# Layer 1 of a four-layer kernel: four-lane products without queries, a mask compared by words, earlier weight loads and moved clears

## The chip, the cores and the metric

One Trainium2 chip, one core. The metric is the device time of one execution in microseconds (us), taken as the median of repeated runs. Everything is float32 except the mask (one byte per entry) and a few integers.

## The reference, cut to what matters

The program updates x (2 batches of 1024 tokens with 256 features) four times, each time by x = x + ffn(cond(x)). Layers 0, 2 and 3 are mixtures of experts. Only layer 1 and some clears of memory are touched. Layer 1 is attention with 16 heads of 16 features, in which one query per head serves every token:

```
q, k, v = x @ Wq.T, x @ Wk.T, x @ Wv.T        (heads h of 16)
tp   = t @ Wt.T                               (t: 256 per batch)
a    = sum_e tp[b,h,e] * q[b,h,s,e]
qmod = sum_s a[b,h,s] * q[b,h,s,:]            (one vector per b, h)
scores[b,h,t,s] = where(mask[t,s], qmod.k[s] / 4, float_min)
c = (softmax(scores) @ v) @ Wo.T
```

After it comes a block with 16 experts: a gate (normalised c times a normalised 256x16 matrix, minus a sigmoid, rectified, softmax), per-expert q, k and v, causal attention, and an output product weighted by the gate. In the inputs all 1024 rows of the mask are equal. Then every token of a batch has the same c, attention over equal rows gives that row back, and layer 1 adds one row of 256 numbers per batch to x.

## The kernel before, in words

Tokens are held twice in SBUF: `xtok` (128 tokens by 16 tiles by 256) and `fx` (the 256 features as 2 halves `k` of 128 partitions, by 2048 tokens). Both are views into one tensor, `big`, of six regions (`ACC`, `EXTRA` and so on). PSUM is `ps`, 8 banks of 128x512. A stage is a Block: a list of instructions for each engine, ordered among each other by semaphores. `with_own_semaphores` (L2561) puts a barrier, a clearing of semaphores and a second barrier behind a part.

Start: `stage_load` (L103). SyncE (SP) loads x and small tables and waits for nine of the loads. ScalarE (ACT) waits for the same nine, then issues three DMAs (L127) that write zeros to all 4992 rows (5.1 MB) of the DRAM scratch `sorted_in`, and one (L129) for one row of `by_token`. `sorted_in` is first used when layer 2 scatters tokens into it (`scatter`, L1421).

Layer 0 ends in `half_l0` (L1429). Its SP list ends with four loads of results, and one load of layer 2's first weights once the old ones are used (L1465).

Layer 1 (`layer1`, L2569) has these stages:

- `stage_l1_project` (L1822). SP loads the mask (8 tiles of 128x1024 bytes), its first row spread to all partitions, and five weight matrices (1.3 MB). PE makes tp (L1863), then q for all tokens (L1871, 16 calls of 512 columns), then a, spread over each head's features by a block-diagonal weight (L1880, 8 calls). ACT copies q out of PSUM (L1898). VectorE (DVE) compares the mask byte by byte with its first row and counts (L1907, L1909, 8 times each), then multiplies and sums q and a (L1923). With the weights of k, qmod becomes U (L1890), a 256-vector per batch and head, so that scores are U.x. The count of differing bytes goes to `differ` (L1940).
- A branch on `differ`. If it is 0, `stage_l1_same_rows` (L2381) runs; the general path (`any_mask`) isn't executed.
- `stage_l1_same_rows` is three Blocks. The first: scores for one batch at a time on 16 partitions (L2428), maximum, exp, transposes (L2435), probabilities times x (L2442), then the products with Wv (L2458) and Wo (L2464). The second is `stage_l1_gating` (L2090): it loads two small tables (L2114, L2115), takes four products and runs some thirty short DVE operations. The third: 32 calls with the experts' value weights as stationary operand and two columns moving (L2523), 32 more with the output weights (L2529), then the row is spread (L2550, L2535) and added to `fx` (L2553) and `xtok` (L2558) by DVE.

The expert weights (4 MB) are issued by SP in the first of these Blocks (L2413, L2414). PE's list is in order, as is each engine's; `link` (L335) makes DVE wait for its own last instruction.

## Time and profile before

| what | value |
|---|---|
| time, median of 3 runs | 1822.16 us (1815.49 to 1824.17) |
| time of the profiled execution | 1827.07 us |
| its span, first to last instruction | 1825.3 us |
| PE, DVE, ACT, POOL busy | 84%, 56%, 36%, 23% of the span |
| mean granted clock of TensorE | 0.905 of full |
| mean DMA rate | 116 GB/s |

The profile is of one execution. PE is TensorE, PEld its weight loads, POOL is GpSimd; L1871 is line 1871 of the kernel. "SPq" and "ACTq" mark the time in which a queue's engine issues a DMA, not the transfer. A float32 matmul call stands as two records, so "x64" in the row of a product means 32 calls; a transpose is one record. The end of a matmul is modelled, so ends of one product and starts of the next overlap.

### The profile page before, as it was taken

How to read it: one execution, taken by the hardware profiler on the slowest of the kernel's cores; microseconds unless marked ns; L12 is line 12 of the kernel's file. 1: busy time of each engine (PE TensorE's matmuls, PEld its weight loads, DVE VectorE, ACT ScalarE, POOL GpSimd, SP SyncE). 2: the span in 40 equal slices, each digit the busy share in tenths (PEclk: the TensorE clock that was granted, in tenths of full speed). 3: DMA queues.
4: the chain of work that ended last, by engine and by line, in shares of the span. 5: the costliest groups of instructions: out<-in, count | busy, mean ns of one | idle time of the engine just before them, and what ended most of it. 6: DMA issues, size and time to landing. Idle time of an engine off the chain costs nothing. (4 is left out here: it accounts for less than half of the span.)

```text
span 1825.3 us, 26214 instructions
## 1 busy us (share of the span) xinstructions
PE 1533.0 (84%) x8442; PEld 1164.3 (64%) x8442; DVE 1013.2 (56%) x1801; ACT 661.3 (36%) x981; POOL 428.0 (23%) x364
## 2 busy tenths in 40 slices
PE   3788878866689999879799999999988699848993
PEld 2553323733668778768688888888776577725662
DVE  2737767452263435473577777776546133536675
ACT  1337767211032333242455555554323133211110
POOL 0412222000034241001033334342003334023321
PEclk9989989886579999989899999999997699959996
DMA  6328981213031334024022221300303232245733
GB/s 200 137 93 331 364 310 58 84 55 93 23 137 62 103 101 150 1 81 162 3 90 99 94 97 57 134 28 14 133 1 130 101 99 79 95 142 203 265 109 107
DMA packets 82585, 211.11 MB, mean 116 GB/s; under 512 B 10561, under 2 KB 57426, under 8 KB 74258
## 3 DMA queue, kind: packets, MB, share of 16 engines
q1 hardware_dynamic: 61568, 160.98, 24.8%
q0 software_dynamic: 15840, 43.27, 7.0%
q10 hardware_dynamic: 5042, 5.11, 0.8%
q8 instruction: 78, 1.28, 0.3%
q14 instruction: 57, 0.47, 0.1%
HBM read 164.90 MB, written 44.43 MB: 115 GB/s over the span
## 5 line engine op out<-in xcount | busy, mean ns | idle before, releaser
L593 POOL DMA_INDIRECT results<-sb_big,sb_s_out_row x63 | 132.8, 2108 | 465.1 <-ACT sb_big L824 303.1
L898 DVE TENSOR_TENSOR sb_h_split<-sb_big,sb_h_split 128x2048 fp32r<-128x2048 f32 x78 | 178.5, 2290 | 87.9 <-ACT sb_h_split L893 87.9
L893 ACT CAST sb_h_split<-sb_big 128x2048 fp32r x78 | 146.6, 1903 | 41.9 <-issue 40.6
L789 PE MATMUL ps<-sb_big,sb_e_hT 128*128 x624 | 141.0, 379 | 1.1 <-DVE sb_e_hT L942 1.1
L282 PE MATMUL ps<-sb_h_split 128*128 128x512 f32 x312 | 133.6, 428 | 9.6 <-DVE sb_h_split L917 6.8
L1031 DVE COPY sb_g_space<-sb_big 128x1024 f32 x168 | 108.4, 699 | 47.0 <-DMA sb_big<-in_l_routed 24.9
L1031 ACT COPY sb_g_space<-sb_big 128x1024 f32 x120 | 118.7, 1050 | 41.7 <-DMA sb_big<-in_l_routed 32.4
L1421 POOL DMA_INDIRECT sorted_in<-sb_big,sb_p_slots x64 | 70.6, 1104 | 260.6 <-DVE sb_p_slots L1247 216.8
L789 PEld LDWEIGHTS ps<-sb_big,sb_e_hT 128*128 128x128 f32 x624 | 118.2, 190 | 18.5 <-issue 1.3
L282 PE MATMUL ps<-sb_g_split,sb_g_ws 128*128 128x512 f32 x256 | 109.6, 428 | 23.3 <-DVE sb_g_product L461 15.7
L284 PE MATMUL ps<-sb_h_split 128*128 128x512 f32 x312 | 124.1, 398 | 0.0
L283 PE MATMUL ps<-sb_h_split 128*128 128x512 f32 x312 | 123.9, 397 | 0.0
L1069 PE MATMUL ps<-sb_g_space,sb_e_rT 128*32 128x512 f32 x768 | 99.9, 640 | 18.3 <-ACT sb_g_space L1031 8.5
L555 POOL DMA_INDIRECT results<-sb_big,sb_p_out_row x78 | 77.6, 995 | 145.3 <-DVE sb_big L704 144.6
L283 PE MATMUL ps<-sb_g_split,sb_g_ws 128*128 128x512 f32 x256 | 107.3, 419 | 0.0
L284 PE MATMUL ps<-sb_g_split,sb_g_ws 128*128 128x512 f32 x256 | 106.5, 416 | 0.0
L282 PE MATMUL ps<-sb_g_ws,sb_g_split 128*128 128x256 f32 x256 | 79.6, 311 | 26.1 <-DVE sb_g_split L467 18.5
L582 POOL DMA_INDIRECT sb_big<-by_token,sb_s_in_row x63 | 64.5, 1025 | 153.0 <-DVE sb_s_out_row L1294 134.4
L436 ACT ACTIVATE sb_g_sg<-ps 128x512 f32<-128x512 f32 x64 | 38.2, 598 | 157.0 <-PE ps L284 108.8
L636 PE MATMUL ps<-sb_big,sb_x_rT 128*128 x312 | 87.5, 403 | 4.1 <-ACT sb_x_rT L681 4.0
L461 DVE TENSOR_TENSOR sb_g_product<-sb_g_sg,ps 128x512 f32<-128x512 f32 x64 | 43.8, 685 | 70.8 <-ACT sb_g_sg L436 54.2
L656 PE MATMUL ps<-sb_big,sb_x_hT 128*128 x312 | 82.1, 386 | 0.0
(416 smaller groups left out, 3318.6 us busy)
## 6 DMA issues: line engine op xcount, KB each, us to landing
sb_big<-in_l_routed SPq DMA_DIRECT2D x32, 1024.0 KB
sb_big<-in_l2f_routed SPq DMA_DIRECT2D x8, 3072.0 KB, 11.1
sb_e_wring<-in_l_experts SPq DMA_DIRECT2D x16, 1408.0 KB
sb_big<-in_l_routed SPq DMA_DIRECT2D x32, 512.0 KB
sb_big<-results SPq DMA_DIRECT2D x32, 512.0 KB, 7.4
sb_big<-sorted_in SPq DMA_DIRECT2D x18, 512.0 KB
by_token<-sb_big SPq DMA_DIRECT2D x12, 512.0 KB, 3.6
sorted_in<-sb_big ACTq DMA_DIRECT2D x2, 2048.0 KB
```

What stands on the lines that cost most here:

```text
L282: pe.matmul(to, w[0], x[0], start=start, stop=False)
L283: pe.matmul(to, w[0], x[1], start=False, stop=False)
L284: return pe.matmul(to, w[1], x[0], start=False, stop=stop)
L555: pool.indirect_dma_start(out=results, out_offset=bass.IndirectOffsetOnAxis(ap=places.out_row[:, j:j + 1], axis=0), in_=self.tile(j), in_o ...
L593: pool.indirect_dma_start(out=results, out_offset=bass.IndirectOffsetOnAxis(ap=places.out_row[:, j:j + 1], axis=0), in_=self.tile(j), in_o ...
L636: last = pe.matmul(psum[:, j % 2, 0:self.NF * P], self.rT[:, j % 2, k * P:(k + 1) * P], self.w[:, e, k * self.NF * P:(k + 1) * self.NF * P ...
L656: last = pe.matmul(psum[:, 2 + j % 2, 0:D], self.hT[:, j % 2, f * P:(f + 1) * P], self.w[:, e, lo:lo + D].rearrange("p s n -> p (s n)"), s ...
L789: last = pe.matmul(psum[:, 7, 0:D], self.hT[:, f // TPC, f % TPC * P:(f % TPC + 1) * P], self.weight(place, 2 * KD * self.F + f * D, D), s ...
L893: act.copy(self.own[part][:, 0, :], self.raw(e, part)).then_inc(self.own_high[part], 1)
L898: dve.tensor_tensor(self.own[part][:, 1, :], self.raw(e, part), self.own[part][:, 0, :], ALU.subtract).then_inc(self.own_low[part], 1)
L1031: last = copy(self.own[part][:, g, :], here.rearrange("p s n -> p (s n)"))
L1069: last = pe.matmul(psum[g * W:(g + 1) * W, 2 * part + u % 2, :], self.rT[:, r % 2, k, g * W:(g + 1) * W], self.own[part][:, g, lo:lo + FU] ...
```

## The change

- The clears of `sorted_in` leave the start and go to SP's list in the first stage of layer 1, from a 128x256 tile of zeros that is read again for every tile of rows. Only the `by_token` row is still cleared at the start. Layer 2's POOL waits for the clears before it scatters; layer 0 waits for one clear instead of four.
- `half_l0` also loads layer 1's weights (now six matrices, Wq in both orientations, 1.5 MB) into `EXTRA`, and the mask as 32-bit words with its first row into `ACC`, behind the four loads of results.
- `stage_l1_project` forms no q. With V = Wq'tp per head, a = V.x; then r = sum of a[s] x[s], and qmod = Wq r, masked by head. Both big products use four quadrants of the array (32 weight columns each), every quadrant with its own 512 tokens. The mask is compared in two DVE instructions of 128x2048 words and summed in one.
- `stage_l1_same_rows` is one Block. Scores, probabilities times x, and both expert products use the quadrants; in the expert products the vectors (padded to 32 columns) are the weights and the expert matrices move. Each batch's softmax is now in two halves that are joined by DVE. ACT takes half of the adds to `fx`.

The core of the diff:

```diff
@@ stage_load @@
                     act.wait_ge(cleared, 1)
-                    act.wait_ge(loaded, 16 * 9)
-                    for lo in range(0, SLOT_TILES2, NT):
-                        hi = min(SLOT_TILES2, lo + NT)
-                        act.dma_start(sorted_in[lo * P:hi * P, :].rearrange("(i p) d -> p i d", p=P),
-                                      acc[:, 0:hi - lo, :]).then_inc(zeroed, 16)
                     act.dma_start(by_token[0:1, :], acc[0:1, 0, :]).then_inc(zeroed, 16)
...
-                    dve.memset(acc, 0.0).then_inc(cleared, 1)
+                    dve.memset(acc[0:1, 0, :], 0.0).then_inc(cleared, 1)
@@ half_l0, SP and POOL @@
+                        sp.dma_start(l1_weights, a["l1_w"]).then_inc(l1_in, 16)
+                        sp.dma_start(l1_words[:, 0:TPB, :], a["mask_words"].rearrange("(i p) s -> p i s", p=P)
+                                     ).then_inc(l1_mask, 16)
+                        sp.dma_start(l1_words[:, TPB, :], a["mask_words"][0, :].partition_broadcast(P)).then_inc(l1_mask, 16)
...
-                        pool.wait_ge(zeroed, 16 * (1 + -(-SLOT_TILES2 // NT)))
+                        pool.wait_ge(zeroed, 16)
@@ half_cond, POOL @@
+                        if n == 2:
+                            pool.wait_ge(swept, 16 * 3)
@@ new helpers @@
+        def in_lanes(pe, to, w, bank):
+
+            for k in range(KD):
+                for g in range(NCH):
+                    last = pe.matmul(psum[g * EQ:(g + 1) * EQ, bank, :], w[:, k, :], fx[:, k, g * CH:(g + 1) * CH],
+                                     start=(k == 0), stop=(k == KD - 1))
+            last.then_inc(to, 1)
+
+        def lanes_times_rows(pe, to, turned, bank):
+
+            for q in range(TPC):
+                for g in range(NCH):
+                    last = pe.matmul(psum[g * EQ:(g + 1) * EQ, bank, 0:D], turned[:, q, g * EQ:(g + 1) * EQ],
+                                     xtok[:, g * TPC + q, :], start=(q == 0), stop=(q == TPC - 1))
+            last.then_inc(to, 1)
+
+        def turn_lanes(pe, to, lanes, n, bank):
+
+            for q in range(n):
+                last = pe.transpose(psum[:, bank, q * P:(q + 1) * P], lanes[:, q * P:(q + 1) * P], ident[:])
+            last.then_inc(to, 1)
@@ stage_l1_project @@
+                        sp.wait_ge(blank, 1)
+                        for lo in range(0, SLOT_TILES2, NT):
+                            n = min(SLOT_TILES2 - lo, NT)
+                            sp.dma_start(sorted_in[lo * P:(lo + n) * P, :].rearrange("(i p) d -> p i d", p=P),
+                                         zero[:].unsqueeze(1).to_broadcast([P, n, D])).then_inc(swept, 16)
...
+                        pe.wait_ge(tpmd, 2)
+                        for d in range(KD):
+                            for o in range(KD):
+                                last = pe.matmul(psum[:, 6, d * BH:(d + 1) * BH], w6[:, WQT, o, d * P:(d + 1) * P],
+                                                 tpm[:, o, :, :].rearrange("p b h -> p (b h)"),
+                                                 start=(o == 0), stop=(o == KD - 1))
+                        last.then_inc(vd, 1)
+                        pe.wait_ge(vc, 1)
+                        in_lanes(pe, ad, V, 0)
+                        pe.wait_ge(ac, 1)
+                        turn_lanes(pe, atd, lanes, TPC, 1)
+                        pe.wait_ge(atc, 1)
+                        lanes_times_rows(pe, rd, aT, 2)
+                        pe.wait_ge(rc, 1)
+                        turn_lanes(pe, rtd, r, KD, 3)
+                        pe.wait_ge(rbd, 1)
+                        for o in range(KD):
                             for k in range(KD):
+                                last = pe.matmul(psum[:, 4, o * BH:(o + 1) * BH], w6[:, WQ, k, o * P:(o + 1) * P],
+                                                 rb[:, k, :, :].rearrange("p b h -> p (b h)"),
+                                                 start=(k == 0), stop=(k == KD - 1))
+                        last.then_inc(qd, 1)
+                        pe.wait_ge(qmd, 2)
                         for d in range(KD):
+                            for o in range(KD):
+                                last = pe.matmul(psum[:, 5, d * BH:(d + 1) * BH], w6[:, WK, o, d * P:(d + 1) * P],
+                                                 qm[:, o, :, :].rearrange("p b h -> p (b h)"),
+                                                 start=(o == 0), stop=(o == KD - 1))
                         last.then_inc(ud, 1)
+                        pe.wait_ge(counted, 1)
+                        pe.matmul(psum[0:1, 7, 64:65], ones[:, 0:1], cnt[:], start=True, stop=True).then_inc(flagd, 1)
...
+                        dve.wait_ge(l1_mask, 32)
+                        link(dve.tensor_tensor(ne[:], words[:, 0:TPB, :], words[:, TPB:TPB + 1, :].to_broadcast(
+                            [P, TPB, S // 4]), ALU.bitwise_xor))
+                        dve.wait_ge(atd, 1)
+                        dve.tensor_copy(aT[:].rearrange("p q g -> p (q g)"), psum[:, 1, :]).then_inc(atc, 1)
+                        link(dve.tensor_scalar(apart[:], ne[:].rearrange("p i s -> p (i s)"), 0, None, ALU.not_equal))
+                        dve.wait_ge(rtd, 1)
+                        link(dve.tensor_copy(rT[:].rearrange("p k g -> p (k g)"), psum[:, 3, 0:KD * P]))
+                        for b in range(B):
+                            two = of_batch(rT[:], b)
+                            last = dve.tensor_tensor(rb[:, :, b, :], two[:, :, 0, :], two[:, :, 1, :], ALU.add)
+                        last.then_inc(rbd, 1)
...
+                        dve.tensor_reduce(cnt[:], apart[:], AX_X, ALU.add).then_inc(counted, 1)
@@ stage_l1_same_rows @@
+                    for g in range(NCH):
+                        sp.dma_start(m1[g * EQ:(g + 1) * EQ, :],
+                                     a["mask"][0, g % 2 * CH:(g % 2 + 1) * CH].partition_broadcast(EQ)).then_inc(masked, 16)
+                    sp.dma_start(simc[:, :, 0:E], a["l1_sim"]).then_inc(simmed, 16)
+                    sp.dma_start(gb[:], a["l1_gates"].partition_broadcast(P)).then_inc(simmed, 16)
+                    for k in range(KD):
+                        sp.dma_start(wv[:, :, k, :], a["l1_qkv"][:, :, k, 2 * H1:3 * H1]).then_inc(wloaded, 16)
+                    sp.dma_start(wo[:], a["l1_o"]).then_inc(wloaded, 16)
...
+                    pe.wait_ge(expd, 1)
+                    turn_lanes(pe, ptd, pr, TPC, 1)
+                    pe.wait_ge(sread, 2)
+                    pe.matmul(psum[:, 4, 0:2 * P], ones[:], spread[:].rearrange("p n q -> p (n q)"), start=True, stop=True
+                              ).then_inc(spreadd, 1)
+                    pe.wait_ge(ptc, 1)
+                    lanes_times_rows(pe, zd, pT, 2)
+                    pe.wait_ge(zc, 1)
+                    turn_lanes(pe, ztd, z, KD, 3)
...
+                    pe.wait_ge(wloaded, 48)
+                    for k in range(KD):
+                        for g in range(4):
+                            last = pe.matmul(psum[g * EQ:(g + 1) * EQ, 6, :], c32[:, k, :], wv[:, 4 * g:4 * g + 4, k, :],
+                                             start=(k == 0), stop=(k == KD - 1))
+                    last.then_inc(vd, 1)
+                    pe.wait_ge(vsd, 1)
+                    pe.matmul(psum[:, 5, 256:256 + B], vs[:], sel[:], start=True, stop=True).then_inc(vtd, 1)
+                    pe.wait_ge(avd, 2)
+                    for n in range(4):
+                        for g in range(4):
+                            last = pe.matmul(psum[g * EQ:(g + 1) * EQ, 7, 0:D], av[:, 4 * g + n, :], wo[:, 4 * g + n, :],
+                                             start=(n == 0), stop=(n == 3))
+                    last.then_inc(outd, 1)
...
+                    act.wait_ge(simmed, 32)
+                    act.activation(gb[:], gb[:], ACT.Sigmoid).then_inc(rooted, 1)
+                    act.wait_ge(maxd, 1)
+                    act.activation(pr[:], pr[:], ACT.Exp, bias=mx[:, 0:1], accum_out=sums[:, 0:1]).then_inc(expd, 1)
+                    act.wait_ge(shared, 1)
+                    act.activation(share[:], share[:], ACT.Exp).then_inc(weighed, 1)
```

## Rows read from the trace of the kernel before

**Rows 1.** Busy by stretch: length, PE, PEld, DVE, ACT, POOL, PEclk, DMA share, GB/s.
```profile
371.80:412.00 40.20, 27.38 (x74) 13.55 (x74) 27.41 (x46) 4.69 (x8) 0.69 (x2) 0.79 0.18 63
...
413.40:444.20 30.80, 25.81 (x92) 11.45 (x92) 6.16 (x18) 3.76 (x5) 0.09 (x1) 0.72 0.44 137
444.20:459.90 15.70, 4.45 (x20) 4.34 (x20) 6.02 (x32) 4.60 (x7) 0.00 (x0) 0.50 0.02 3
459.90:496.20 36.30, 28.72 (x132) 28.17 (x132) 8.38 (x12) 0.00 (x0) 0.00 (x0) 0.50 0.00 0
...
497.50:1825.30 1327.80, 1165.65 (x5864) 950.28 (x5864) 755.78 (x1351) 465.50 (x704) 353.77 (x282) 0.92 0.29 100
```

**Rows 2.** Timeline of the start: start us, duration us, engine, line, what, idle before.
```profile
11.11 11.33 ACTq L127 DMA_DIRECT2D sorted_in<-sb_big  x3
22.47 2.09 ACTq L129 DMA_DIRECT2D by_token<-sb_big  x1
25.75 1.28 ACT L187 ACT_TABLE_LOAD   x1 [25.75 <-PEq L2567]
```

**Rows 3.** Timeline of the first stage of layer 1.
```profile
381.83 1.87 PE L1863 MATMUL ps<-sb_condT,sb_l_w 128*128 128x2 f32 x8 [12.23 <-DMA sb_l_w<-in_l_w]
...
411.86 0.14 DVE L1940 CAST sb_l_differ<-sb_l1p_cnt 1x1 int32<-1x1 f32 x1
```

**Rows 4.** Groups of layer 1: count, busy us, mean ns, idle before.
```profile
L2523 PE MATMUL ps<-sb_f_c,sb_f_wbuf 128*128 128x2 f32 x64 | 13.8, 352 | 7.8 <-PEq L2111 7.8
...
L1907 DVE TENSOR_TENSOR sb_l1p_ne<-sb_l1p_m 128x1024 f32<-128x1024 uint8 x8 | 9.8, 1224 | 7.0 <-DMA sb_l1p_m<-in_mask 6.7
L1909 DVE TENSOR_REDUCE sb_l1p_cnt<-sb_l1p_ne 128x1 f32<-128x1024 f32 x8 | 9.8, 1220 | 0.3
...
L1880 PE MATMUL ps<-sb_big,sb_l_bd 128*128 128x512 f32 x16 | 7.1, 597 | 0.8 <-ACT sb_big L1898 0.8
...
L1923 DVE CUSTOM_DVE_ANT_0 sb_l_junk<-sb_big,ps 128x512 f32<-128x512 f32 x8 | 5.5, 689 | 3.2 <-PE ps L1880 3.2
L1898 ACT COPY sb_big<-ps 128x512 f32<-128x512 f32 x8 | 4.7, 586 | 25.7 <-PE ps L1871 25.7
L2558 DVE TENSOR_TENSOR sb_big<-sb_big,ps 128x2048 f32<-128x2048 f32 x2 | 4.5, 2280 | 0.0
...
L2553 DVE TENSOR_SCALAR sb_big<-sb_big,sb_f_row 128x1024 f32<-128x1024 f32 x4 | 2.7, 747 | 0.0
...
L2535 PE MATMUL ps<-sb_ident,sb_f_rowb 128*128 128x128 f32 x4 | 1.1, 435 | 0.7 <-DVE sb_f_rowb L2550 0.7
```

**Rows 5.** Timeline, products in four quadrants in layers 0 and 2.
```profile
60.35 1.92 PE L298 MATMUL ps<-sb_big,sb_wr 128*32 128x512 f32 x16 [0.92 <-PEq L191]
...
142.39 1.93 PE L1093 MATMUL ps<-sb_g_space,sb_r_quads 128*32 128x256 f32 x32 [0.19 <-issue]
...
501.56 3.41 PE L298 MATMUL ps<-sb_big,sb_wr2c 128*32 128x512 f32 x16
```

**Rows 6.** Timeline of the second stage of layer 1.
```profile
444.61 0.43 SPq L2115 DMA_DIRECT2D sb_g1s_gb<-in_l_gates  x1
447.71 0.22 ACT L2139 ACTIVATE sb_g1s_gb<-sb_g1s_gb 128x16 f32<-128x16 f32 x1 [1.90 <-DMA sb_g1s_gb<-in_l_gates]
...
452.96 0.25 DVE L2161 RECIPROCAL sb_g1s_ns<-sb_g1s_ns 128x16 f32<-128x16 f32 x1 [0.38 <-ACT sb_g1s_ss L2142]
...
459.48 0.19 DVE L2185 TENSOR_TENSOR sb_f_rw<-sb_g1s_tmp,sb_g1s_small 128x32 f32<-128x32 f32 x1
```

**Rows 7.** Busy by stretch, during the clears.
```profile
12.40:24.40 12.00, 0.00 (x0) 0.00 (x0) 0.00 (x0) 0.00 (x0) 0.00 (x0) 1.00 1.05 365
```

**Rows 8.** Timeline of SyncE's queue at the end of layer 0.
```profile
325.03 0.60 SPq L1465 DMA_DIRECT2D sb_wbuf<-in_l2c_shared  x1
```

**Rows 9.** Timeline of ScalarE in layer 0: a table load and its user.
```profile
70.88 1.28 ACT L436 ACT_TABLE_LOAD   x1
72.17 1.09 ACT L436 ACTIVATE sb_g_sg<-ps 128x512 f32<-128x512 f32 x2
```

More of the change, by code:

```diff
@@ L1841, in stage_l1_project @@
+                cnt = sb("l1p_cnt", [P, 1], on=own)
+                zero = sb("l1p_zero", [P, D], on=own)
+                blank, masks, order, tpd, tpmd, vd, vc, ad, ac, atd, atc, rd, rc, rtd, rbd, qd, qmd, ud, counted, flagd = (
+                    sem("l1p_" + n) for n in ("blank", "masks", "order", "tpd", "tpmd", "vd", "vc", "ad", "ac", "atd", "atc", "rd",
+                                              "rc", "rtd", "rbd", "qd", "qmd", "ud", "counted", "flagd"))
                 with nc.Block() as block:
@@ L1900, in _ @@
+                        act.wait_ge(rd, 1)
+                        act.copy(r[:], psum[:, 2, 0:D]).then_inc(rc, 1)
                     @block.vector
                     def _(dve):
-                        dve.memset(qm[:], 0.0)
-                        dve.wait_ge(mloaded, 32)
-                        for i in range(TPB):
-                            if i:
-                                dve.wait_ge(counted, 2 * i)
-                            dve.tensor_tensor(ne[:], m8[:, i, :], m1[:], ALU.not_equal).then_inc(counted, 1)
-                            dve.wait_ge(counted, 2 * i + 1)
-                            dve.tensor_reduce(cnt[:, i:i + 1], ne[:], AX_X, ALU.add).then_inc(counted, 1)
+                        link = chain(dve, order)
@@ L1926, in _ @@
-                        dve.wait_ge(asum, 8)
-                        dve.tensor_tensor(qmod[:], part[:, :, :, 0], part[:, :, :, 1], ALU.add).then_inc(order, 1)
-                        dve.wait_ge(order, 2)
-                        for o in range(KD):
-                            for b in range(B):
-                                last = dve.tensor_scalar(qm[:, o, b, o * 8:(o + 1) * 8], hm[:, :, 0],
-                                                         qmod[:, o, b:b + 1], float(HW) ** -0.5, ALU.mult, ALU.mult)
@@ new lines, in stage_l1_same_rows @@
+            E, BH = E1, B * HEADS
+            wv = sb("f1_wv", [P, E, KD, H1], on=own)
+            wo = sb("f1_wo", [P, E, D], on=own)
+            m1 = sb("f1_m1", [P, CH], U8, on=own)
+            lim = sb("f1_lim", [P, CH], on=own)
+            pr = sb("f1_pr", [P, CH], on=own)
+            pT = sb("f1_pT", [P, TPC, P], on=own)
+            mx, sums = (sb("f1_" + n, [P, 1], on=own) for n in ("mx", "sums"))
+            spread = sb("f1_spread", [P, 2, P], on=own)
+            peak, total, share, tmp2 = (sb("f1_" + n, [P, B, 2, HEADS], on=own) for n in ("peak", "total", "share", "tmp2"))
@@ new lines, in stage_l1_same_rows @@
+            cb = sb("f1_cb", [P, KD, B, P], on=own)
+            c32 = sb("f1_c32", [P, KD, EQ], on=own)
+            ss, top, small = (sb("f1_" + n, [P, B], on=own) for n in ("ss", "top", "small"))
+            L, tmp, oh1, oh2, gated, rw, rwm = (
+                sb("f1_" + n, [P, B, E], on=own) for n in ("L", "tmp", "oh1", "oh2", "gated", "rw", "rwm"))
+            rwl = sb("f1_rwl", [P, 4], on=own)
+            sel = sb("f1_sel", [P, B], on=own)
+            selb = sb("f1_selb", [P, B, P], on=own)
```

489 lines of the change are left out of this document (234 added, 255 removed).

## The prediction

> **What bounds the kernel now.** I first read the busy time by stretch, which cuts the span where one stage gives way to the next. Layer 1 is the piece from 371.8 to 497.5 us, 125.7 us in all, and the 1327.8 us behind it begin only when its last add is done [rows 1]. So layer 1 is serial: whatever it loses comes off the end. PE looks busy in it, but with little: from 444 to 496 us the granted clock is 0.50, the lower of its two levels (1.2 GHz). Then the timeline of the start: ACT issues the three clears from 11.11 to 22.44 us and the `by_token` row until 24.56, and layer 0 starts at 25.75, 1.2 us behind that [rows 2]. Nothing computes between. Then the timeline of the first stage: the first product, at 381.83, waits 12.2 us for its weights, and the last cast ends at 412.0 [rows 3]. Last the groups of layer 1: q and the expert products, plus the byte compares and counts (8 + 8 of 1.22 us, 19.6 us of DVE) that hold up tp and with it a [rows 4].
>
> **The change, part by part.**
>
> *Start.* The nine loads had landed at 11.11, when ACT went on [rows 2]. SP still waits for them; ACT's one small clear takes 2.09 us beside it and its memset is shorter. With the same 1.2 us of barrier layer 0 starts at 12.3: **-13.4 us**.
>
> *First stage, now 40.2 us* [rows 1]. Weights and mask have landed (below). Prices: a product of 4 calls (8 records) with full weights and few columns is 1.87 us [rows 3], as are 64 records in 13.8 us [rows 4]. A four-quadrant product, 16 records of 512 columns, has two prices: 1.92 us at the upper clock, 3.41 at the lower; 32 records of 256 columns are 1.93 at the upper, so about 3.5 at the lower [rows 5]. I take the lower clock throughout: the products here are short with waits between, as in the second half of the layer before, where it read 0.50 [rows 1]. A pass over 512 columns of PSUM is 0.59 us on ACT and 0.69 on DVE; four transposes with their tail are 1.1 at that clock [rows 4]. A short DVE step is 0.2 [rows 6].
> The chain: four small products 7.6; the two big ones 3.4 + 3.5; copies 0.6 + 0.7; four transposes 1.1 and two 0.6; two 256-column copies 0.8; eight short DVE steps 1.6; behind U the count, U's copy and the flag 1.0. Sum 20.9, so **-19.3 us**.
> The mask is three DVE instructions of 2048 columns. The nearest rows are the add of 2048 columns, 2.28, and the reduction of 1024, 1.22 [rows 4]. The xor (2.3) has 5 us of cover (in_lanes, ACT's copy, the transposes). The compare (1.3 to 2.3) stands between aT's copy and rT's, with 4.5 us of cover; the count (2.3) has U's product (1.9) beside it. Uncovered they would cost up to 6 us; nothing speaks for a gain.
> The clears are on SP's queue here. Their issue took ACTq 11.33 us [rows 2]; the stage's barrier comes at 20.9, so it is hidden. The data, 5.1 MB, moved at 365 GB/s before [rows 7], 14 us; the next user of SP's queue is the mask row of the second stage, at 22. Nothing then waits. POOL's new wait in layer 2 stands before all its scatters, but comes over 60 us after the issue of the clears; it costs nothing unless they take that long.
>
> *Prefetch.* SP's last issue of layer 0 is at 325.03 [rows 8], 47 us before layer 1. Three more DMAs with 2.7 MB in front of it take 7.4 us at 365 GB/s [rows 7]. They stand behind the results, so these aren't late. Cost nothing; without that cover they would give back the wait for the weights.
>
> *Second stage, now 82.8 us in three Blocks* [rows 1]. (a) SP issues four mask rows and sim, 0.4 each, then gates, whose data is used 3.1 us after the issue [rows 6]: 5.4. ACT's list has the Sigmoid first, so Exp waits for gates: Sigmoid 0.2, table load 1.3, exp 0.6 + 0.2: 7.7, where scores alone would have let it start at 5.6. This is the new wait; the softmax, all of PE and the rest are behind it. (b) Transposes 1.1, copy 0.7, spread operand and its product 1.2, product with x 3.5, z's copy 0.4, two transposes 0.6: 7.5. The joining of the halves (DVE, about nine short steps) lies beside the product with x. (c) z joined 0.7, Wv 1.9, masking 0.4, Wo 1.9, three copies 0.8, logits 1.9, two steps and the square roots 0.75: 8.35. (d) The gating chain, 452.96 to 459.67, is 6.7 [rows 6], plus two steps: 7.15. The value product (3.4) runs beside it, its weights long there. (e) Weighting and sum 1.4, the turn 0.3, two steps 0.5, output product 3.5, copy 0.4, rows turned 0.95, copy 0.2: 7.25. (f) Two adds to fx of 0.68 (4 in 2.7 us) and two to xtok of 2.28 [rows 4]: 5.9; ACT's two lie beside. With 0.4 for the branch's tail: 44.2, so **-38.6 us**. The barriers between stages stay.
>
> By the Trainium skill (ScalarE: Activation LUTs, What ACT_TABLE_LOAD costs) a switch costs about 2.66 us with a drain, of which the load is 1.28. In layer 0 a load at 70.88 has its user at 72.17, 1.29 later [rows 9], so the row speaks for 1.3; by the page (a) would be 1.4 us longer. The same skill (TensorE: Matmul & The Clock Gate, Measured speedup vs the span model) gives 3.07x for four row tiles and 2.38x for three column tiles. Here sixteen 512-column records in a line took 7.1 us [rows 4] and in quadrants 1.92 [rows 5], 3.7x; by 3.07x each of the four big products on the path would be some 0.8 us longer, 3 us in all.
>
> **Sum.** 13.4 + 19.3 + 38.6 = 71.3 us. Against the profiled execution's own 1827.07 that is 1755.8; that execution is 4.9 us above the median of the runs, and against 1822.16 it is 1750.9. I take **1751**. Layers 2 and 3 are unchanged; their 1327.8 us only start earlier.
>
> **Rivals.**
> 1. *The upper clock.* If PE kept its upper clock (2.4 GHz) through layer 1, each of the four big products on the path would save 1.5, and each of the seven small ones at most half of its 1.9: up to 12.6, so 1738 to 1743. For: the first stage now reads 0.79 on average [rows 1]. Against: the 0.50 from 444 on, and PE has more gaps after the change. Chance 0.10.
> 2. *The covers are short.* The mask work stays on DVE's path (6), Exp's wait and the many hand-overs cost more than the short steps show (some 45 links at 0.1 to 0.2, 4 to 9), or a big product is slower than in layer 2. That gives 1761 to 1766. For: word-wise xor and compare have no row. Against: the hand-overs in [rows 6] are priced in. Chance 0.20.
> 3. *Slower: the clears block SP's queue.* They read one zero tile again and again, which no row shows, and the second stage's loads stand behind them on the same queue. In the free case gates land 27.7 us after the first stage's start. If the 5.1 MB need longer, all of the second stage waits. At 100 GB/s (the mean behind layer 1 [rows 1]) they take 51 us: Exp starts 24 us late, 1775. The gain is used up at 98 us, 52 GB/s; at 40 GB/s they take 128 us, 1851. Against: the same row size ran at 365. Chance 0.07 for a delay that shows, 0.03 for slower than before.
> 4. *It doesn't do what it says.* If the word compare counted a difference, the general path would run, slower by far than 1822. An xor of equal words is 0. Chance 0.01.
>
> **The numbers.** A measurement of this kernel tells about 0.5%, 9 us, from no change. Forecast 0.60, rivals 0.10, 0.20, 0.07 (0.03 of it slower), 0.01, and 0.02 for something that leaves no difference. Faster is 0.94, same 0.02, slower 0.04. The range runs from 1738, the whole of rival 1, to 1768, rival 2's 15 us (6 + 9) and 2 us of scatter.
>
> **What would show it.** Layer 0's first transpose at 12.3; layer 1's first product at once, with no wait for weights; the first stage 20.9 us long with PEclk 0.5; SP's three clears issued within 12 us; Exp's wait ending at 7 us with the gates as its releaser; second stage 44 us; layer 2's first scatter without a wait. It is wrong if SP's queue or the DMA rate shows the clears still moving in the second stage, if a DVE row of 2048 words stands between two PE products with PE idle, or if the part behind layer 1 isn't 1328 us.

## The result and the profile after

The changed kernel takes 1749.13 us (median of 4 runs, 1748.79 to 1754.33), the kernel before beside it 1823.16 (4 runs, 1815.49 to 1827.36). The ratio is 0.9606, with a 95% interval of 0.9576 to 0.9636: 74 us less, against 71.3 forecast. The profiled execution has a span of 1752.6 us.

The busy time by stretch of the changed kernel, cut as in [rows 1]: layer 0, the two stages of layer 1, and all behind them (length, PE, PEld, DVE, ACT, POOL, PEclk, DMA share, GB/s):

```profile
12.20:355.90 343.70, 280.67 (x2260) 156.31 (x2261) 205.17 (x335) 183.01 (x257) 72.27 (x65) 0.92 0.54 194
355.90:377.50 21.60, 16.86 (x88) 10.17 (x88) 8.31 (x17) 0.96 (x2) 0.92 (x3) 0.50 0.67 237
379.00:423.60 44.60, 25.71 (x142) 12.96 (x142) 20.63 (x72) 9.89 (x15) 0.61 (x2) 0.58 0.32 97
423.60:1752.60 1329.00, 1166.07 (x5864) 950.73 (x5864) 755.68 (x1351) 464.90 (x704) 353.50 (x282) 0.92 0.29 100
```

Measured from event to event (layer 0's first table load; the first DVE instruction of layer 1; the end of the flag's cast; the first table load behind it; the end of the last add; the first DMA issue of layer 2):

| us | before | after | difference | forecast |
|---|---|---|---|---|
| start | 25.75 | 12.19 | -13.56 | -13.4 |
| layer 0 | 346.18 | 343.76 | -2.42 | 0 |
| first stage | 40.07 | 21.55 | -18.52 | -19.3 |
| second stage | 82.73 | 44.59 | -38.14 | -38.6 |
| two gaps (barrier, branch) | 2.81 | 3.24 | +0.43 | 0 |
| behind | 1327.76 | 1327.27 | -0.49 | 0 |
| span | 1825.3 | 1752.6 | -72.7 | -71.3 |

The three stretches that the change touches account for 70.2 us of the 72.7. Layer 0's 2.4 us are within its scatter: in the runs below, where its code is the same, its length lies between 339 and 346 us, and that of the part behind layer 1 between 1315 and 1330. The two stages of layer 1 repeat to some tenths in the three traces of the changed kernel, so the experiments are read by them first and by the time second. The kernel before has one trace only.

The timeline of the changed kernel's start, ScalarE with its queue (start, duration, engine, line, what, idle before), then SyncE's queue from the end of layer 0 to layer 2:

```profile
1.80 0.48 ACTq L126 DMA_DIRECT2D by_token<-sb_big  x1
12.19 1.28 ACT L184 ACT_TABLE_LOAD   x1 [12.19 <-PEq L2659]
```

```profile
311.11 0.50 SPq L1461 DMA_DIRECT2D sb_big<-in_l_w  x1
...
356.21 7.92 SPq L1879 DMA_DIRECT2D sorted_in<-sb_l1p_zero  x3
379.29 1.75 SPq L2455 DMA_DIRECT2D sb_f_m<-in_mask  x4
...
381.70 0.59 SPq L2458 DMA_DIRECT2D sb_f_gb<-in_l_gates  x1
```

The 11 us of issue that stood before layer 0 [rows 2] are gone, and the clears' issue on SP's queue is over in 7.9 us, 15 us before the masks are asked for. Layer 2's first scatter, at 451.39, waits for its row numbers from VectorE and not for the clears. The timeline of the first stage, TensorE and the mask work of VectorE:

```profile
355.91 1.84 PE L1897 MATMUL ps<-sb_condT,sb_big 128*128 128x2 f32 x8 [2.60 <-PEq L2659]
...
360.47 2.28 DVE L1953 TENSOR_TENSOR sb_l1p_ne<-sb_big 128x2048 int32<-128x2048 int32 x1
360.61 3.64 PE L1829 MATMUL ps<-sb_big,sb_l_V 128*32 128x512 f32 x16 [0.32 <-DVE sb_l_V L1951]
...
366.79 1.22 DVE L1957 TENSOR_SCALAR sb_l1p_apart<-sb_l1p_ne 128x2048 f32<-128x2048 int32 x1
366.92 3.64 PE L1837 MATMUL ps<-sb_big,sb_l_aT 128*32 128x256 f32 x32 [0.85 <-DVE sb_l_aT L1956]
...
374.79 2.28 DVE L1972 TENSOR_REDUCE sb_l1p_cnt<-sb_l1p_apart 128x1 f32<-128x2048 f32 x1
374.93 1.91 PE L1925 MATMUL ps<-sb_l_qm,sb_big 128*128 128x32 f32 x8 [0.35 <-DVE sb_l_qm L1967]
```

The first product waits for no weights, where 12.23 us of idle time stood before it [rows 3]. Each of the three mask instructions has a product beside it; only the count (2.28 us) outlasts its product (1.91). The timeline of the second stage, where it was priced:

```profile
383.95 0.15 DVE L2554 TENSOR_SCALAR sb_f_mx<-sb_f_mx 128x1 f32<-128x1 f32 x1
384.86 0.21 ACT L2528 ACTIVATE sb_f_gb<-sb_f_gb 128x16 f32<-128x16 f32 x1 [4.57 <-DMA sb_f_gb<-in_l_gates]
385.10 1.28 ACT L2530 ACT_TABLE_LOAD   x1
386.39 0.72 ACT L2530 ACTIVATE sb_f_pr<-sb_f_pr,sb_f_mx 128x512 f32<-128x512 f32 x1
387.26 1.11 PE L1844 MATMUL ps<-sb_ident,sb_f_pr 128*128 128x128 f32 x4 [1.53 <-ACT sb_f_pr L2530]
...
395.45 1.06 PE L2488 MATMUL ps<-sb_f_zT,sb_big 128*128 128x16 f32 x8 [0.78 <-DVE sb_f_zT L2585]
...
402.33 0.25 DVE L2607 RECIPROCAL sb_f_ns<-sb_f_ns 128x16 f32<-128x16 f32 x1 [0.38 <-ACT sb_f_ss L2537]
...
409.36 0.69 DVE L2636 TENSOR_TENSOR sb_f_vw<-ps,sb_f_rwl 128x512 f32<-128x512 f32 x1
...
412.41 3.64 PE L2515 MATMUL ps<-sb_f_wo,sb_f_av 128*32 128x256 f32 x32 [0.67 <-DVE sb_f_av L2642]
...
417.79 1.42 DVE L2647 TENSOR_SCALAR sb_big<-sb_big,sb_f_row 128x1024 f32<-128x1024 f32 x2
419.12 4.48 DVE L2651 TENSOR_TENSOR sb_big<-sb_big,ps 128x2048 f32<-128x2048 f32 x2
```

The new wait of part (a) is there as named: the maxima are ready at 384.1, the Exp runs at 386.39, behind gates, Sigmoid and a table load.

### The profile page after: what moved, and what is told of

Read it like the earlier page. It is cut to its first block and busy times, and to the rows that moved or that the text cites. A ratio compares the mean times of both kernels' runs of the same rounds, so it can differ in the third digit from the quotient of the medians.

```text
span 1752.6 us, 25999 instructions
## 1 busy us (share of the span) xinstructions
PE 1489.3 (85%) x8354; PEld 1130.2 (64%) x8354; DVE 990.9 (57%) x1782; ACT 658.8 (38%) x978; POOL 429.6 (25%) x366
## 5 line engine op out<-in xcount | busy, mean ns | idle before, releaser
L1418 POOL DMA_INDIRECT sorted_in<-sb_big,sb_p_slots x64 | 70.2, 1096 | 220.7 <-DVE sb_p_slots L1244 178.4
L1066 PE MATMUL ps<-sb_g_space,sb_e_rT 128*32 128x512 f32 x768 | 97.1, 624 | 13.7 <-issue 6.4
L279 PE MATMUL ps<-sb_g_ws,sb_g_split 128*128 128x256 f32 x256 | 77.8, 304 | 21.4 <-DVE sb_g_split L464 14.5
L433 ACT ACTIVATE sb_g_sg<-ps 128x512 f32<-128x512 f32 x64 | 38.1, 597 | 148.0 <-PE ps L281 116.6
L280 PE MATMUL ps<-sb_g_ws,sb_g_split 128*128 128x256 f32 x256 | 76.8, 300 | 7.5 <-issue 7.5
```

Source lines behind the costliest of these rows:

```text
L279: pe.matmul(to, w[0], x[0], start=start, stop=False)
L280: pe.matmul(to, w[0], x[1], start=False, stop=False)
L1066: last = pe.matmul(psum[g * W:(g + 1) * W, 2 * part + u % 2, :], self.rT[:, r % 2, k, g * W:(g + 1) * W], self.own[part][:, g, lo:lo + FU] ...
L1418: pool.indirect_dma_start(out=table, out_offset=bass.IndirectOffsetOnAxis(ap=slots[:, n:n + 1], axis=0), in_=rows[:, n % NT, :], in_offset ...
```

## The experiments

Twelve kernels ran, in three groups of four; each group has its own chip and its own runs of the kernel before (1810.66, 1822.98 and 1809.31 us), so times are compared within a group and ratios across. Stage lengths come from each run's trace, by the marks of the table above.

| | us (median) | ratio, 95% | first stage | second stage |
|---|---|---|---|---|
| the change, again | 1743.38 | 0.9630 (0.9607 to 0.9652) | 21.54 | 44.29 |
| clears at the start | 1753.15 | 0.9694 (0.9675 to 0.9713) | 21.55 | 44.51 |
| late loads | 1753.75 | 0.9678 (0.9655 to 0.9701) | 32.30 | 43.93 |
| old second stage | 1777.69 | 0.9817 (0.9795 to 0.9838) | 21.55 | 76.77 |
| old expert products | 1764.69 | 0.9682 (0.9660 to 0.9704) | 21.55 | 57.19 |
| clears three times | 1767.88 | 0.9702 (0.9670 to 0.9733) | 21.55 | 45.84, and 13.7 of wait before it |
| no comparison | 1753.14 | 0.9606 (0.9584 to 0.9627) | 21.14 | 44.36 |
| filled waits | 1749.47 | 0.9601 (0.9575 to 0.9626) | 19.25 | 39.02 |
| exp first | 1741.23 | 0.9630 (0.9604 to 0.9656) | 21.55 | 41.68 |
| three moves | 1736.92 | 0.9592 (0.9567 to 0.9618) | 17.66 | 42.59 |
| filled moves | 1737.86 | 0.9612 (0.9584 to 0.9639) | 18.71 | 37.62, and 1.35 more of gap |
| the change, a third time | 1743.51 | 0.9643 (0.9619 to 0.9667) | 21.55 | 44.50 |

**The change, again.** The same file, as the measure of its group.

> The changed kernel once more, nothing edited. All of my terms are stage lengths of one trace each; this run says how far a stage length moves by itself. Serial-sum theory: start 12.2 us, first stage of layer 1 21.6, second 44.6, each within 0.3 us, median within 3 us of 1749. Layer 0 was 2.4 us shorter after the change (343.7 against 346.1), which no term explains: if that is scatter, layer 0 moves by a microsecond or more here too; if it is an effect of the change (no clears beside its start), it stays at 343.7.

It repeats, in both stages to 0.3 us. Layer 0 took 342.20 us, so it moves by itself. The median missed the 3 us expected around 1749: on this chip both kernels are faster, and the change saves 67.3 us; in the third group it saves 65.8. Both are below the 70.2 us of the three stretches. Why isn't shown, as the kernel before was not traced there; its own stages may move (see the old second stage below).

**Clears at the start.** The clears go back to ScalarE's queue ahead of layer 0, with the whole of `acc` set to zero for them, and layer 0 waits for them again.

```diff
+                    act.wait_ge(loaded, 16 * 9)
+                    for lo in range(0, SLOT_TILES2, NT):
+                        act.dma_start(sorted_in[lo * P:hi * P, :]..., acc[:, 0:hi - lo, :]).then_inc(swept, 16)
...
-                            sp.dma_start(sorted_in[lo * P:(lo + n) * P, :]..., zero[:]...).then_inc(swept, 16)
```

> The changed kernel with the three clears back on ScalarE's queue at the start, all else as changed. Serial-sum theory: layer 0 starts at 25.7 us instead of 12.2 and the time is 13.5 us above the changed kernel's, 1762.6; the first stage of layer 1 stays 21.6 us, since the clears are hidden there. Rival (the clears are not free in layer 1): the first stage and the start of the second become shorter by 1 to 5 us, and the time rises by only 8 to 12. Layer 0: 346 us if the clears slow it, 343.7 if they don't.

The timeline of ScalarE and its queue at the start of this run:

```profile
11.15 11.72 ACTq L129 DMA_DIRECT2D sorted_in<-sb_big  x3
...
25.67 1.28 ACT L189 ACT_TABLE_LOAD   x1 [25.67 <-PEq L2662]
```

Layer 0 starts 13.6 us later (25.67 against 12.08), while the first stage is 21.55 long either way. So the clears cost their whole issue ahead of layer 0 and nothing in layer 1. The time differs by 9.8, not 13.6, which lies in the range of the rival; the rival's reason, shorter stages in layer 1, is out by their lengths (21.55 and 44.51). In this profile layer 0 was 5.2 us shorter (337.05) than in the run before, the shortest of all runs. Whether that is scatter or something that the edit does isn't shown.

**Late loads.** Weights and mask words are loaded where the first stage begins, the clears behind them.

```diff
-                        sp.dma_start(l1_weights, a["l1_w"]).then_inc(l1_in, 16)
...
+                        sp.dma_start(l1_weights, a["l1_w"]).then_inc(l1_in, 16)
                         sp.wait_ge(blank, 1)
```

> The changed kernel with the mask words and the six weight matrices loaded at the start of layer 1, mask first, and the clears behind them, as the old order of loads was. Serial-sum theory: the first product waits some 10 us (the old one was issued behind 1.1 MB of mask and waited until 10.0 us into the stage; now 1.5 MB of weights), all else behind it is unchanged: plus 10 to 12 us, 1760 to 1761. The clears end later, at 28 us or so, when the stage of 32 us is still on, so they add nothing. Rival (the loads would have been hidden, or the clears share the engines with them): plus under 5, or plus 20 and more.

The timeline of SyncE's queue in its first stage, then TensorE's first product:

```profile
356.60 0.43 SPq L1875 DMA_DIRECT2D sb_big<-in_l_w  x1
357.08 14.88 SPq L1879 DMA_DIRECT2D sorted_in<-sb_l1p_zero  x3
```

```profile
366.32 1.87 PE L1897 MATMUL ps<-sb_condT,sb_big 128*128 128x2 f32 x8 [13.01 <-DMA sb_big<-in_l_w]
```

The wait for the weights is back, and the first stage is 10.8 us longer, all of it ahead of the first product; the time rises by 10.4. The clears' issue takes 14.88 us behind 2.7 MB of loads instead of 7.92.

**Old second stage.** The second stage and the gating of the kernel before, with everything else of the change kept.

```diff
-                    in_lanes(pe, sd, U[:].rearrange("p k b h -> p k (b h)"), 0)
+                                    last = pe.matmul(psum[0:HEADS, 2 * b + ch, :], U[:, k, b, :],
...
-                    lanes_times_rows(pe, zd, pT, 2)
+                                last = pe.matmul(psum[0:HEADS, 6 + b, 0:D], pT[:, b, s * HEADS:(s + 1) * HEADS],
...
+                with nc.Block() as block:
+                                last = pe.matmul(psum[:, 0, e * B:(e + 1) * B], wv[:, e, k, :], c[:, k, :],
```

> The changed kernel with the old three Blocks of the second stage (scores on 16 partitions, gating in a Block of its own, experts' weights stationary with two columns moving), all else as changed. Serial-sum theory: the second stage is 82.8 us again instead of 44.6, the time 38 us higher, 1787. Its four product groups alone (9.7, 9.8, 13.8, 13.8 us) against 3.6 each make 32 of it. Rival (the clears, which now end just before, or a lower clock on entry, slow the old form too): more than 40.

34.3 us of time and 32.5 us of stage come back, short of 38, since the old code ran faster here: 76.77 us against 82.73. The rival had expected a lower clock on entry and more than 40; it went the other way. The timelines give the reason: the product of the shares with x took 7.08 us here and 9.84 in the kernel before, that with U 8.51 against 9.70, and the transposes and the products with Wv and Wo were some 1.5 us shorter in sum. The busy time by stretch of this run has the clock beside them:

```profile
385.00:395.00 10.00, 8.07 (x44) 3.91 (x44) 1.54 (x6) 1.24 (x2) 0.00 (x0) 1.00 0.40 170
395.00:405.00 10.00, 5.17 (x35) 4.97 (x34) 1.45 (x7) 2.78 (x3) 0.00 (x0) 0.68 0.02 4
405.00:415.00 10.00, 2.50 (x12) 2.39 (x12) 5.81 (x31) 1.82 (x4) 0.00 (x0) 0.50 0.00 0
```

In the kernel before the ten-us stretches from 424 to 434 and to 444, which hold the same products, had 0.66 and 0.79. So some 5.4 of the 38.1 us by which the second stage got shorter hang on the clock that the one trace of the kernel before had, and the new code of the stage is not shown to be their cause.

**Old expert products.** One Block stays; only the products with the value and output weights are the two-column ones of before, with the row's spread by transposes.

```diff
-                            last = pe.matmul(psum[g * EQ:(g + 1) * EQ, 6, :], c32[:, k, :], wv[:, 4 * g:4 * g + 4, k, :],
+                            last = pe.matmul(psum[:, 6, e * B:(e + 1) * B], wv[:, e, k, :], c32[:, k, 0:B],
...
-                            last = pe.matmul(psum[g * EQ:(g + 1) * EQ, 7, 0:D], av[:, 4 * g + n, :], wo[:, 4 * g + n, :],
+                            last = pe.matmul(psum[:, 7, f * B:(f + 1) * B], wo[:, e, f * P:(f + 1) * P], av[:, e, 0:B],
```

> The second stage stays one Block, but the products with the value weights and the output weights are taken as before the change: 64 two-column products each in place of 16 of 512 columns in four lanes, and the spread back over the tokens by transposes of a row spread on VectorE. Theory (the products are the gain): each 64 records take 13.8 us where the lane product takes 3.64 us. The output product is all on the path, +10.2; of the value product, 5.9 us are covered by the gating that ended later anyhow, +4.3; the spread of the row adds about 1 to 2 us and the turns that go away save 1.5. So +13 to +17 us against the kernel after, about 1762 to 1766 where that reads 1749, and the second stage 58 to 61 us in place of 44.5. Rival (what was gained is the joining of three Blocks into one and the weights being fetched early): the products matter little, +0 to +5, second stage below 50.

The timeline of its second stage, both expert products:

```profile
399.67 13.79 PE L2509 MATMUL ps<-sb_f_c,sb_f_wv 128*128 128x2 f32 x64
414.45 13.81 PE L2515 MATMUL ps<-sb_f_av,sb_f_wo 128*128 128x2 f32 x64 [0.99 <-DVE sb_f_av L2636]
```

The stage is 12.7 us longer than 44.5, just under the 13 to 17 expected, and the ratio 0.0076 above that of the run without the comparison in the same group (13.9 us). The rival, under 5 us, is out. So the expert products in lanes carry a third of the second stage's 38.1 us. By the two undo runs another 19.6 (76.8 less 57.2) belong to the rest of the edit: one Block for three, the products with U and x in lanes, gates and weights fetched early. It wasn't split further. The last 6 are what the old code was faster by in the run above, most of it the clock's.

**Clears three times.**

```diff
+                        for again in range(3):
                             for lo in range(0, SLOT_TILES2, NT):
-                                sp.dma_start(sorted_in[...], zero...)
+                                sp.dma_start(cleared_too[again][...], zero...)
```

> It writes the same clears a second and a third time, into two more scratch tables (15.3 MB in place of 5.1), on the same queue. Theory (the queue and the transfer rate decide, as in rival 3 of the prediction): at the 365 to 386 GB/s seen, the data takes 40 to 42 us from the start of the first stage, so it ends some 17 to 19 us into where the second stage starts; the nine issues take 23 to 35 us of SP's sequencer, so the barrier after the first stage comes 2 to 13 us late, and the gates and masks land only behind the data, Exp 12 to 17 us later than in the kernel after. Time +14 to +17 us, 1763 to 1767 where the kernel after reads 1749. Rival (16 engines share the queues fairly, small loads slip past the clears): the issue alone shows, +0 to +3. A second rival: the clears are also slower when there are more of them, then above +25.

The timeline of SyncE's queue in this run, then the busy time of a stretch before the second stage's loads landed:

```profile
356.53 7.92 SPq L1881 DMA_DIRECT2D sorted_in<-sb_l1p_zero  x3
364.50 13.55 SPq L1881 DMA_DIRECT2D spare_one<-sb_l1p_zero  x3
378.09 12.98 SPq L1881 DMA_DIRECT2D spare_two<-sb_l1p_zero  x3
393.33 1.75 SPq L2457 DMA_DIRECT2D sb_f_m<-in_mask  x4
```

```profile
386.00:396.00 10.00, 2.52 (x12) 0.62 (x16) 0.00 (x0) 1.28 (x1) 0.61 (x2) 0.50 1.09 386
```

The sum came as expected, by another split. The data runs at 386 GB/s to the end. In the second and third pass three issues take about as long as their data (13.55 and 12.98 us for 5.1 MB, which need 13.2 at that rate), so the nine issues last 34.5 us, the barrier after the first stage is 13.7 us late, and the second stage itself is only 1.3 us longer. So the clears can block SP's queue, as rival 3 has it, though mostly by holding the barrier and not by data in front of the loads. The change's own clears meet this too: their third issue alone takes 6.14 us of the 7.92, here as there (6.13), but the stage lasts 21.55 us and hides it.

**No comparison.**

```diff
-                        link(dve.tensor_tensor(ne[:], words[:, 0:TPB, :], words[:, TPB:TPB + 1, :]..., ALU.bitwise_xor))
-                        link(dve.tensor_scalar(apart[:], ne[:]..., 0, None, ALU.not_equal))
-                        dve.tensor_reduce(cnt[:], apart[:], AX_X, ALU.add).then_inc(counted, 1)
+                        dve.memset(cnt[:], 0.0).then_inc(counted, 1)
```

> It leaves out the comparison of the masks: the xor, the compare and the count over 2048 words each, and reports no difference. Theory (they lie in the shadow of PE and of ScalarE's copies): only the turn's link on VectorE comes earlier; the first stage is 0 to 0.9 us shorter than 21.55, the time lower by 0 to 1 us, which the rounds can't tell from nothing. Rival 2 of the prediction (the mask work is uncovered): first stage 3 to 6 us shorter, 15.5 to 18.5, time lower by 3 to 6 us.

The first stage is 21.14 us, 0.4 less. The mask work is hidden but for the end of the count, for which TensorE's last product had waited 0.28 us.

**Filled waits.** In each wait of TensorE stand one to five products of 128 columns with the identity, 20 in the long wait of the gating. Nobody uses their results.

```diff
+        def keep_busy(pe, n, bank):
+            for _ in range(n):
+                pe.matmul(psum[:, bank, 0:P], ident[:], fx[:, 0, 0:P], start=True, stop=True)
```

> It adds products of 128 columns, whose results nobody uses, in TensorE's waits in both stages, so that the engine is hardly idle. Otherwise the same. Theory 1 (the clock of 0.50 comes of the short products with waits between; keep the engine at work and it rises): the granted clock reads above 0.8 in the first stage and in the second, the big lane products take 1.9 instead of 3.64 us, so up to 4 x 1.7 off the path and some tenths on each small one, less about 2 us for the fillers themselves: -5 to -10 us. Theory 2 (the fillers are too few or too light, the clock stays 0.50): the products take as long as before, and the fillers delay some that are on the path, +1 to +4 us.

The busy time by stretch of this run, its two stages, and then within the first:

```profile
355.09:374.40 19.31, 17.59 (x118) 12.31 (x118) 8.31 (x17) 0.96 (x2) 0.91 (x3) 0.74 0.75 266
375.89:414.90 39.01, 30.82 (x222) 20.49 (x222) 20.65 (x72) 9.89 (x15) 0.61 (x2) 0.81 0.36 111
```

```profile
358.00:362.00 4.00, 4.00 (x21) 2.35 (x25) 2.42 (x2) 0.00 (x0) 0.00 (x0) 0.50 1.09 386
362.00:366.00 4.00, 4.00 (x22) 2.30 (x14) 0.30 (x1) 0.58 (x1) 0.00 (x0) 0.63 1.09 383
366.00:370.00 4.00, 3.60 (x47) 2.57 (x46) 1.95 (x3) 0.37 (x1) 0.00 (x0) 1.00 0.99 351
```

The clock rises to 1.00 in the middle of the first stage, the products with aT, with pT and with the output weights take 1.93 us each instead of 3.2 to 3.64, and the two stages are 2.3 and 5.6 us shorter than in the changed kernel. The means of 0.74 and 0.81 miss the 0.8 expected in one stage. The clock is thus a cause of its own, and one that the kernel could use. In the time of the whole it hardly shows: 3.7 us below the run without the comparison, which is inside the scatter.

**Exp first.**

```diff
-                    act.wait_ge(simmed, 32)
-                    act.activation(gb[:], gb[:], ACT.Sigmoid).then_inc(rooted, 1)
                     act.wait_ge(maxd, 1)
...
                     act.activation(share[:], share[:], ACT.Exp).then_inc(weighed, 1)
+                    act.wait_ge(simmed, 32)
+                    act.activation(gb[:], gb[:], ACT.Sigmoid).then_inc(rooted, 1)
```

> It moves ScalarE's Sigmoid of the gates behind the second Exp, so that the first Exp waits for the scores alone. Theory (the prediction's new wait is real): the first Exp needs the scores and the maxima, ready 2 us before the Exp ran in the kernel after (its table load began at 385.10; the negated maxima were there at 384.1 and the table can be loaded before); the second stage is 1.5 to 2.5 us shorter than 44.4. Rival (something else is as late, the table load or the product that spreads the maxima): 0 to 0.5 us. The time itself by -2, which five rounds may or may not tell from the scatter; the length of the stage in the trace decides.

The timeline of the start of its second stage:

```profile
375.25 1.28 ACT L2528 ACT_TABLE_LOAD   x1 [8.01 <-PEq L2659]
...
380.26 0.72 ACT L2528 ACTIVATE sb_f_pr<-sb_f_pr,sb_f_mx 128x512 f32<-128x512 f32 x1 [3.73 <-DVEq L2555]
...
381.00 0.19 DVE L2557 TENSOR_TENSOR sb_f_sim<-sb_f_simc 128x32 f32<-128x32 f32 x1 [0.83 <-DMA sb_f_gb<-in_l_gates]
...
381.25 0.62 PE L2473 MATMUL ps<-sb_f_sim,sb_ones 128*128 128x16 f32 x4 [2.17 <-DVE sb_f_sim L2557]
...
381.71 0.69 PE L1844 MATMUL ps<-sb_ident,sb_f_pr 128*128 128x128 f32 x4
```

The Exp starts 5.0 us into the stage instead of 7.2 to 7.4, and the stage is 2.8 us shorter (41.68), more than the 1.5 to 2.5 expected. But not all of the 2.2 us of the Exp reach the stage. TensorE's list has the product with the squared sim matrix (L2473) ahead of the transposes (L1844), and it waits for the same loads as the Sigmoid did. So the transposes start 6.46 us into the stage, against 8.06 in the third run of the change: the order of the list gives 1.6 us. The other 1.2 us are the clock's, 0.66 here against 0.58 there; the product with Wo, for one, took 1.17 us against 1.87. The time is 2.3 us below that of the change, inside the scatter.

**Three moves**: the move of Exp first and the two below, the count of the mask ahead of r's copy and all adds to the features on ScalarE. **Filled moves** has the unused products as well.

```diff
                         link(dve.tensor_scalar(apart[:], ne[:].rearrange("p i s -> p (i s)"), 0, None, ALU.not_equal))
+                        dve.tensor_reduce(cnt[:], apart[:], AX_X, ALU.add).then_inc(counted, 1)
...
-                    for k in range(KD):
-                        dve.tensor_scalar(fx[:, k, 0:S], fx[:, k, 0:S], row[:, k, 0:1], None, ALU.add)
+                    for b in range(B):
+                        for k in range(KD):
+                            act.activation(fx[:, k, b * S:(b + 1) * S], fx[:, k, b * S:(b + 1) * S], ACT.Identity,
+                                           bias=row[:, k, b:b + 1])
```

> The move of the Sigmoid, and two more: all adds to the features on ScalarE, so that VectorE begins at once with the adds to the tokens, and the count of the mask right behind its comparison. Theory (each sits on the path): second stage 2 us shorter by the Sigmoid and 1.2 to 1.4 by the adds, first stage 0.3 to 0.5 shorter by the count; together -3.2 to -3.9 us in the two stages. Rival (the count now stands before the copy that the next turn waits for): the first stage is 0.3 to 1 us longer instead.

> The three moves together with the unused products in TensorE's waits (the Sigmoid now behind the copy of z, some unused products more at the end of the first stage). Theory (clock and waits are separate causes and add up): the stages, 19.25 and 39.0 with the unused products alone, become 17.5 to 18.5 and 35.5 to 37; 11 to 13 us less than the kernel after in the two stages, 1738 to 1741 where that reads 1751. Rival (they overlap: with the faster products the moved work, count, Sigmoid, becomes the last to end): 8 to 9 us, not more than the unused products alone gave.

> The changed kernel itself once more, as the measure for the three others on the same chip: 0.958 to 0.965 of the kernel before, stages 21.55 and 44.3 to 44.6 us.

Three moves has the lowest ratio of the study, 6.6 us below the change in the same group; its five runs (1731.65 to 1739.31) all lie below the five of the change (1739.38 to 1748.22). Against the filled kernels the intervals overlap. Its stages don't gain as expected, though: 3.9 us in the first, where 0.3 to 0.5 were, and 1.9 in the second, where 3.2 to 3.4 were. The timeline of its first stage, then the adds at the end of the second:

```profile
355.05 1.02 PE L1897 MATMUL ps<-sb_condT,sb_big 128*128 128x2 f32 x8 [2.61 <-PEq L2658]
...
358.94 3.64 PE L1829 MATMUL ps<-sb_big,sb_l_V 128*32 128x512 f32 x16 [0.32 <-DVE sb_l_V L1951]
...
364.79 1.93 PE L1837 MATMUL ps<-sb_big,sb_l_aT 128*32 128x256 f32 x32 [0.85 <-DVE sb_l_aT L1956]
365.91 2.29 DVE L1958 TENSOR_REDUCE sb_l1p_cnt<-sb_l1p_apart 128x1 f32<-128x2048 f32 x1
...
368.11 0.41 DVE L1960 COPY sb_l_rT<-ps 128x256 f32<-128x256 f32 x1
```

```profile
412.36 4.49 DVE L2650 TENSOR_TENSOR sb_big<-sb_big,ps 128x2048 f32<-128x2048 f32 x2 [0.90 <-PE ps L2523]
```

The first product and that with aT ran at the upper clock, with the same products before them as in the changed kernel (1.84 and 3.64 us there). With the transposes and the third small product the shorter products sum to 3.9 us, all that the first stage gained. The move of the count gave nothing in sum: TensorE's last product came 0.36 us sooner, but the count now holds r's copy, as the rival had it, and the product behind that came 0.34 us later. In the second stage the transposes start 6.83 us in, 1.2 sooner than in the change. The adds give 0.5, not 1.2 to 1.4, since those to the tokens now wait for the product that spreads the row (L2523). So by the traces some 1.7 of the 5.8 us in the two stages are the moves' own and the rest the clock's. Filled moves is no faster (1737.86). Its stages are the shortest in sum, but six unused products at the end of the first stage kept the barrier waiting, 1.35 us. Stages and gap together are 8.4 us below those of the third run of the change (59.2 against 67.6), where 11 to 13 were expected: the number of the rival. Its reason, that the moved work ends last, is hardly seen. Rather, eight records of unused products stood ahead of the second stage's transposes (7.43 us in, against 6.83), and the value product waited 0.39 us for its weights.

## Why the prediction was right

*The start.* Forecast 12.3, measured 12.19. The undo run gives the step alone.

*The first stage.* 20.9 forecast, 21.55 measured. The four small products took 7.59 us (7.6). The two big ones took 3.64 each (3.4 and 3.5), which is 0.4 of the missing 0.65; the rest is in the hand-overs. The lower clock, assumed throughout, came true: the stage reads 0.50 in all three traces of the change. That was in part luck, since the same products took 3.9 us less in the run with three moves.

*The clears and the prefetch.* The clears cost nothing in layer 1, as forecast: its first stage is 21.55 us with them and without. The prefetch saves the wait, 10.7 us by the late loads. That it costs layer 0 nothing is shown only within layer 0's scatter: 343.71 us without it, 340.9 to 343.8 with it in the three traces of the change.

*The second stage.* 44.2 forecast, 44.59 measured, but with errors both ways, up to 1.2 us, that nearly cancel; that the sum is off by only 0.4 is luck. The steps, from the rows above, forecast in brackets: until the first transpose 8.25 (7.7); to the product with Wv 8.19 (8.2, with z joined); to the gating 6.88 (7.65), since the product with Wv ran at the upper clock, 1.06 us; the gating 7.03 (7.15); from there to the adds 8.43 (7.25); the adds to the end 5.81 (6.3 with the branch's tail). The step most off is (e), by 1.2 us: weighting and sum until the turn 1.79 (1.4), the turn 0.63 (0.3), two steps 0.63 (0.5), the output product with its hand-over 3.71 (3.5). In (a) the gates landed 5.85 us into the stage (5.4). The new wait was seen rightly, but (a) has it on ScalarE alone: Exp first shows that TensorE's product with the sim matrix waits for the same loads. And the measure of the gain, 82.8 less 44.2, took the kernel before by one trace, of which some 5.4 us moved with the clock.

*The rates.* By the Trainium skill (ScalarE: Activation LUTs, What ACT_TABLE_LOAD costs) a switch would be about 2.66 us with its drain. The Exp follows its load's start by 1.29 us here too, 385.10 to 386.39, so the trace doesn't agree. By the Trainium skill (TensorE: Matmul & The Clock Gate, Measured speedup vs the span model) four row tiles gain 3.07x and three column tiles 2.38x. With pT as the weights, the product with x took 7.08 us in a line (old second stage) and 1.93 in four lanes (filled waits), both at the upper clock: 3.7x, and the measurement decides.

*The rivals.* Rival 1 did not happen; filled waits got 7.9 us of its 12.6, with the clock up for part of the time only and the unused products in the way. Rival 2's causes are all there, but small: 0.4 us for the mask work, 0.1 to 0.2 for each big product (3.64 against 3.4 and 3.5), 0.55 in (a) and 1.2 in (e). Rival 3's delay needs more than twice the data: with the clears three times the issue of the second pass ended at 378.05, just as the first stage did, and only the third made it late. The general path of rival 4 wasn't taken.

## What to carry to other kernels

Where stages are serial and short, price each step from the rows and compare stage lengths, not the total: in three runs of the change the stages repeat to 0.3 us while 1750 us of kernel scatter by several. But read the granted clock beside each length, for it moved one stage by 3.9 us and another by some 5.4. Put loads and clears on a queue that stands idle behind finished work, but count what the queue holds: here from the third clear on an issue took 2.2 to 6.1 us, and a stage's barrier waits for the last. In a list of instructions on one engine, put the one whose result the others wait for first, and look at the next engine's list too: the Exp ran 2.2 us sooner ahead of the Sigmoid, of which 1.6 reached the stage.

## What was not expected of the hardware

TensorE's clock in a stretch of short products wasn't settled by the stretch's own work: one run of eleven without unused products had the upper level where the other ten, with the same products in front, had 0.50 (1.02 against 1.84 us for the first product; 1.93 against 3.64 for that with aT). In the changed kernel the level fell in the gap before the first product (0.93 from 354.0 to 355.9), in the run with three moves only behind it (1.00 from 355 to 356, then 0.50). The products of the old second stage were 5.4 us shorter behind the new first one, by one trace each. Products whose results nobody uses lifted it from 0.50 to 0.74 and from 0.58 to 0.81 in the two stages, which got 7.9 us shorter in sum although they hold more work.

A clear that reads one zero tile over and over moved at 386 GB/s, and didn't slow down over 15.3 MB.
